# An attention and experts block on one core: another layout for a weighted sum, and another order in its drain

## The reference

```
y    = clip(modulated_linear(x), -256, 256)              # weights scaled by the batch's condition
x1   = x + (y + attention(y))                            # 16 heads of 64, 4 groups of keys and values
kx   = modulated_linear(x1)                              # reshaped to 16 heads of 8 features
A    = softmax(kx kx^T / sqrt(8))                        # within one token: 16 x 16 over the heads
tok  = modulated_linear(A kx)
out  = x1 + sum over the top 2 of 8 experts of gate_e * (relu(tok W1_e + b1_e) W2_e + b2_e)
```

## Time and profile before

| | |
|---|---|
| median of 3 runs | 598.16 us (595.11 to 598.86) |
| the profiled execution | 596.94 us, span 595.1 us |
| busy in the span | PE 575.1, PEld 492.3, DVE 483.7, ACT 372.0, POOL 288.1 us |
| one steady slot | 14.17 us (pair begins at 298.63 and at 312.80) |
| slots 33 and 34, routing, first expert | from about 480 to 514.80 us |
| experts | 514.80 us to the end |

### The profile page before, as it was taken

How to read it: one execution, slowest core, us unless ns; L and a number is a source line. 1 busy time by engine, 2 the same in 40 slices (tenths; PEclk the granted TensorE clock), 3 DMA queues, 4 the chain that set the end, 5 groups by cost and what they waited for, 6 DMA issues and landing times. The chain is left out here.

```text
span 595.1 us, 15251 instructions
## 1 busy us (share of the span) xinstructions
PE 575.1 (97%) x4516; PEld 492.3 (83%) x4516; DVE 483.7 (81%) x1026; ACT 372.0 (63%) x855; POOL 288.1 (48%) x248
## 2 busy tenths in 40 slices
PE   8999999999999999999999999999998997799998
PEld 8888888888888888888888888888887896466775
DVE  4235888898989898988889898989898788777776
ACT  1767767777777677777777767777775321534443
POOL 1011666666666666666666666666666563000000
PEclk9999999999999999999999999999999977999999
DMA  7300000000000000000000000000000000000004
GB/s 240 86 2 2 1 3 2 0 0 0 0 0 0 0 0 0 0 0 0 0 0 0 0 0 0 0 0 0 0 0 2 1 1 0 1 1 0 0 0 141
DMA packets 9364, 7.18 MB, mean 12 GB/s; under 512 B 1089, under 2 KB 8833, under 8 KB 9217
## 3 DMA queue, kind: packets, MB, share of 16 engines
q1 hardware_dynamic: 9344, 6.94, 3.9%
HBM read 4.84 MB, written 2.10 MB: 12 GB/s over the span
## 5 line engine op out<-in xcount | busy, mean ns | idle before, releaser
L1068 POOL TENSOR_TENSOR pair<-kx 128x1152 f32<-128x1152 f32 x32 | 82.2, 2568 | 167.4 <-DVE shifted L388 158.4
L580 PE MATMUL bank_a<-v,prob 128*128 128x65 f32 x1024 | 128.5, 274 | 1.5 <-ACT prob L814 0.8
L580 PEld LDWEIGHTS bank_a<-v,prob 128*128 128x128 f32 x1024 | 121.8, 192 | 6.3 <-ACT prob L814 3.2
L1063 POOL TENSOR_TENSOR mix_hi<-mix_hi 128x512 f32<-128x512 f32 (+2 forms) x96 | 116.8, 1217 | 7.5
L271 DVE TENSOR_REDUCE row_max<-bank_s 128x4 bf16<-128x512 f32 x128 | 88.9, 694 | 26.2 <-PE bank_s L555 25.3
L814 ACT ACTIVATE prob<-bank_t 128x512 f32<-128x512 f32 x128 | 68.9, 589 | 6.9 <-PE bank_t L570 4.7
L587 PE MATMUL misc<-yT,wq_sb 128*128 128x128 f32 x512 | 69.6, 279 | 0.5 <-DVE yT L419 0.5
L570 PE MATMUL bank_t<-qT,kT 64*128 64x256 f32 x512 | 65.7, 376 | 0.0
L1056 POOL TENSOR_TENSOR mix_hi<-weight,kx 128x1024 f32<-128x1024 f32 x32 | 64.1, 2002 | 3.1 <-ACT weight L814 3.1
L282 DVE TENSOR_TENSOR att<-bank_a,recip_den 128x256 f32<-128x256 f32 x128 | 54.4, 425 | 13.0
L587 PEld LDWEIGHTS misc<-yT,wq_sb 128*128 128x128 f32 x512 | 62.0, 191 | 3.6 <-DVE yT L419 0.7
(11 more groups left out here) (149 smaller groups left out, 998.9 us busy)
## 6 DMA issues: line engine op xcount, KB each, us to landing
out<-acc_all SPq DMA_DIRECT2D x8, 256.0 KB, 2.3
x_all<-in_xT SPq DMA_DIRECT2D x1, 1024.0 KB, 9.7
w_sb<-in_w SPq DMA_DIRECT2D x2, 512.0 KB
x_all<-in_xT SPq DMA_DIRECT2D x1, 768.0 KB, 7.5
wq_sb<-in_wq SPq DMA_DIRECT2D x1, 512.0 KB, 6.1
wpost_sb<-in_wpost SPq DMA_DIRECT2D x1, 512.0 KB, 9.6
x_all<-in_xT SPq DMA_DIRECT2D x1, 256.0 KB, 3.3
b_rows<-in_b SPq DMA_DIRECT2D x16, 4.0 KB
```

The lines of the kernel that those rows point to most:

```text
L580: last = mm(att_bank(g)[:, w, :], prob[:, g % 2, w, :], v1[:, j, g, :], start=(w == 0), stop=True, skip_group_check=True)
L1063: G.tensor_tensor(mix_hi[:, 0:r, :], mix_hi[:, 0:r, :], mix_hi[:, r:2 * r, :], ALU.add).then_inc(s_hi, 1)
L1068: G.tensor_tensor(pair[:, :, :], bass.AP(kx2, jc * 2 * P, [[4 * P, P], [0, SHIFTS], [1, P]]), bass.AP(kx2, jc * 2 * P, [[4 * P, P], [MD, S ...
```

## The change

On VectorE the product of the mixing is written transposed: `mix_lo` is now laid out as (feature, shift), so that the 8 terms of one sum lie next to each other and each write is 8 floats behind the last. One reduction over them (`mix_part`) takes the place of the three additions. GpSimd's `mix_hi` gets two buffers, and its product waits for the mix_sum of two batches before instead of one.

In the late slots VectorE does the scores of h first, and copies them itself with two reductions of length 1 (`own_copies`) where ScalarE had two copies. The first choice of the early tiles moves from slot 33 to slot 34, behind the last mixing, and ScalarE's route_exp with it; the second choice of the early tiles is no longer made apart, but with the recent ones over all 32. Of TensorE's fillers, keep_going(12) in slot 34 becomes keep_going(4), and three keep_going(3), in slots 33 and 34, go away; keep_going(40) in slot 33 stays.

```diff
-        mix_lo = sb("mix_lo", [P, MH // 2, P])
-        mix_hi = sb("mix_hi", [P, MH // 2, P])
+        mix_lo = sb("mix_lo", [P, P, MH // 2])
+        mix_part = sb("mix_part", [P, P])
+        mix_hi = sb("mix_hi", [P, 2, MH // 2, P])
...
-                    V.tensor_tensor(mix_lo[:, :, :].rearrange("p r (h e) -> p r h e", e=MD),
+                    V.tensor_tensor(mix_lo[:, :, :].rearrange("p (h e) r -> p r h e", e=MD),
                                     weight[:, jd, 0:MH // 2, :].unsqueeze(3).to_broadcast([P, MH // 2, MH, MD]),
                                     bass.AP(kx2, jd * 2 * P, [[4 * P, P], [MD, MH // 2], [MD, MH], [1, MD]]),
                                     ALU.mult).then_inc(s_lo, 1)
                 if D:
-                    dve.wait_ge(s_lo, 4 * d + 1)
-                    V.tensor_tensor(mix_lo[:, 0:4, :], mix_lo[:, 0:4, :], mix_lo[:, 4:8, :], ALU.add).then_inc(s_lo, 1)
+                    dve.wait_ge(s_lo, 2 * d + 1)
+                    V.tensor_reduce(mix_part[:, :], mix_lo[:, :, :], AX.X, ALU.add).then_inc(s_lo, 1)
...
-                    V.tensor_tensor(mix_lo[:, 0:2, :], mix_lo[:, 0:2, :], mix_lo[:, 2:4, :], ALU.add).then_inc(s_lo, 1)
-                    V.tensor_tensor(mix_lo[:, 0, :], mix_lo[:, 0, :], mix_lo[:, 1, :], ALU.add).then_inc(s_lo, 1)
...
+                def own_copies():
+                    if H:
+                        dve.wait_ge(s_score, n(h))
+                        V.tensor_reduce(score[:, 1:MH // 2, MH:2 * MH], score[:, 1:MH // 2, 0:MH].unsqueeze(3), AX.X,
+                                        ALU.max).then_inc(s_twice, 1)
+                        dve.wait_ge(s_twice, n(h))
+                        top = MH // 2 - 1
+                        V.tensor_reduce(score[:, SHIFTS:MH, 0:MH],
+                                        bass.AP(score, top * (2 * MH - 1) + MH,
+                                                [[2 * MH * MH, P], [-(2 * MH - 1), top], [1, MH], [1, 1]]),
+                                        AX.X, ALU.max).then_inc(s_mirror, 1)
+
                 if late(s):
                     head_scores()
+                    own_copies()
                     head_shift()
-                    mixed()
-                    if s == BATCH + 2:
-                        second_choice(EARLY, 1)
...
-                if s_is(s, BATCH + 1):
+                if s_is(s, BATCH + 2):
                     dve.wait_ge(s_log, 1)
                     dve.wait_ge(s_const, 3)
                     first_choice(EARLY)
...
-            second_choice(RECENT, 2)
+            second_choice(range(BATCH), 2)
...
                     if s_is(s, BATCH + 2):
-                        keep_going(12)
+                        keep_going(4)
...
-                if late(s):
-                    keep_going(3)
...
                 if s_is(s, BATCH + 2):
-                    keep_going(3)
                     gate_logits(RECENT[-1:])
...
                 if late(s):
-                    head_copies()
                     head_weights()
-                if s_is(s, BATCH + 1):
-                    route_exp(EARLY)
...
                     f(mixT[:, :], misc[2][:, 0, :], scale=style[:, 2, bass.ds(d, 1)]).then_inc(s_mixT, 1)
+                if s_is(s, BATCH + 2):
+                    route_exp(EARLY)
...
-                    need(pool, s_msum, n(d - 1))
+                    need(pool, s_msum, n(d - 2))
```

## The result

The changed kernel takes 606.89 us (median of 4 runs, 606.2 to 609.13), the one before 598.09 us. The ratio is 1.0164, with a 95% interval of 1.0139 to 1.019: slower by 1.6%, and outside the predicted range. The profiled execution took 606.25 us, with a span of 604.4 against 595.1.

A forecast was written before the change was run, and what follows sets the result against it. TensorE was taken to bound the loop, and a chain over VectorE the drain. Loop 0, drain -3.8 and clock +1.6 gave -2.2 us, so 596.0 us from a median of 598.16; range 592.3 to 603 for 8 in 10 runs.

The forecast's parts named there:

- part 1: VectorE's mixing: rows written next to each other, one 1.21 us reduction for additions of 2.67 us, gaining VectorE 1.46 us a slot.
- p = 0: VectorE's product: p is the extra time for writing with a step of 8 floats, taken as 0, range 0 to 0.76 us.
- The first rival: VectorE's product in every slot: strided writes are slow, TensorE waits from p = 0.55 us; 603.8 us at 0.76, chance 0.25.
- slack of 0.15 us: Steady slot: prob's first half ends at 307.9, TensorE needs it at 308.20, leaving about 0.15 us after the hand-over.
- The loop's gain: Steady slots: VectorE's saving hardly shows because GpSimd's half becomes late; put at 0, from nothing to 0.05 us a slot.
- The drain: Late slots: new order and shorter sum end mix(31) at 496.9 instead of 501.37, a gain of 4.5 us.
- From mix(31) to count: Transposition, logits and routing after the last mixing: 6.9 to 7.5 us instead of 6.70, so 0.2 to 0.8 lost.
- the net up to count: Drain up to the routing's count: the earlier mix(31) less the longer routing, a net gain of 3.8 us.
- The clock: Experts: with fewer fillers TensorE may start at half clock for 0 to 6.8 us, costing 0 to 3.2, taken as 1.6.
- the loop as a gain: Loop: rival that TensorE did wait for VectorE, 0.2 us a slot, total 590.4 us; chance 0.08.
- a drain without effect: Drain: rival that mix(31) is no earlier and a cold start eats the rest, 598 to 600 us; chance 0.08.
- the forecast's own case: Whole kernel with p = 0: the product's write costs nothing extra, time 596.0 us; chance 0.42 for 594.3 to 598.

The follow-up runs named there:

- the experiment with x_all first: Changed kernel with the new x_all placed between VectorE's product and its reduction, against the kernel before: 598.05 us, ratio 1.0008.
- pairs: Changed kernel with two shifts next to each other, product written with a step of 2 floats, against the kernel before: 596.7 us, ratio 0.9983.
- the drain alone: Changed kernel with the product and three additions of before turned back, against the kernel before: 597.09 us, ratio 0.9988.
- the old order with the reduction: Kernels with the drain order of before and the one reduction; the one with only the new layout and reduction took 605.5 us, ratio 1.0139.
- old order with x_all first: Kernel before with the transposed product, the one reduction and x_all between them, nothing of the new drain order: 596.27 us, ratio 0.9979.
- both kernels with idle fillers and x_all first: Eleven fillers where TensorE waits, added to the x_all-first kernels, against the kernel before: new drain order 596.75 us, old order 595.72 us.

## Why the prediction was wrong

**The step that failed** is in part 1: "I take p = 0 and keep 0.76 for the range." The trace had one pair of rows on accesses of this step, the reductions of the earlier trace rows, and they gave 0.76 us. I set them aside because they are reads, and had no row that says that writes are different. They are not: 2.00 against 1.23 us alone, so p = 0.77, and 0.81 in the loop (2.32 against 1.51), at and above the top of my 0 to 0.76. The rule that I cited spoke on the same side. The nearest row should have been the value, and "it is a write" the reason for the other end.

**The first rival was right in its place and too small in its price.** It named the chain x_all, x1s, prob, and the experiment with x_all first shows that this is the way. It had TensorE waiting from p = 0.55 on, 0.22 us a slot at 0.76, 6.3 us in all. The slot grew by 0.35 and the 30 slots by 9.3. The place was the only one, but the slack of 0.15 us in front of it was mis-read: by the weight load it was 0.03, as worked out above, and that tenth in 29 slots is about the 3 us by which its total of 603.8 was short. Its sign, x1s that delays prob, is what the trace has; TensorE's busy share, 99.38 for 99.58, hardly showed it.

**The loop's gain** of 0 to 0.05 us a slot for the 1.46 us that VectorE would save with a fast product is right: 14.08 before, 14.09 with the sum at full speed. mix_sum waits for GpSimd instead, as said.

**The drain.** Forecast 4.5 us for mix(31) with p = 0. Measured from the last pair product it is 3.34 in the changed kernel, where two slow products cost 1.6, and 4.8 with pairs. With the slot ahead of it (12.44 us before, 11.98 with pairs) it is 5.3: near, and on the safe side. The blocks by GpSimd fell where I had laid them. From mix(31) to count, forecast 0.2 to 0.8 us longer, measured 1.31. The transposition starts 0.53 us after mix(31), as forecast, and from the logits to count it is 4.42 us, as forecast (1.16 + 3.2). From the transposition to the logits it is 3.05 us at half clock, where I had the 2.39 of before; I had put the price of the clock on the experts alone. With pairs the net up to count is 26.8 - 23.4 = 3.4 us, and 3.9 with the slot ahead, where I had 3.8.

**The clock.** Forecast 1.6 us at the experts for a cold stretch of 0 to 6.8; the stretch came, 3.4 us long, and cost 1.4: the first expert matmul to the first addition of its result is 7.85 us against 6.45. The other 1.0 of the 2.39 isn't the clock (last section). Why the experts begin at half clock here is open: in the kernel with x_all first, where TensorE has the same instructions, they begin at full clock (6.44 us).

**The rivals that fell**: the loop as a gain, and a drain without effect.

**Luck in the forecast's own case.** 596.7 us with pairs lies near 596.0, but the terms don't all agree. The 1.6 us for the clock at the experts did not come there (6.45 us to the first addition), and 1.0 us that nobody had forecast, at full clock, stood in its place. By the stages of the trace the kernel with pairs gains 2.5 us behind the first pair product; the medians give 0.9.

## What to carry to other kernels

Before a transposed write is put on a path that counts, work out how many elements share 16 bytes: two float32 in a line are free, one alone in its line costs 0.62 to 0.75 ns more on VectorE here, reading or writing, and a layout in pairs keeps both sides at full speed. When an engine of 99% busy is the bound, look at the count of its instructions in a stretch and not at its busy time, and at everything that stands behind the edited instructions on their own engine: the loss came through an addition of 0.28 us that the change didn't touch. When you read a slack in front of a matmul, read it to the load of its weights. A row that gives a price for the nearest thing is the value to take; only another row is a reason to take zero.

## What the runs showed that I had not expected

The experts' stage has the same instructions in all kernels, and still takes 80.3 us before and in the drain alone, 80.9 in the old order with the reduction, and 81.3 in the new order with it. In the kernel with pairs the clock is full over it:

```profile
521.00:560.00 39.00, 38.40 (x211) 26.73 (x212) 27.64 (x86) 16.97 (x33) 0.00 (x0) 1.00 0.00 0
```

The chain that ended last goes over TensorE there before (bank_t 6% of the span, VectorE's acc_all 0%). After, most of it does too, but VectorE's additions and its sequencer (DVEq) have 1% each:

```profile
PE bank_t L783 5%; PE misc L791 3%; PE bank_s L791 2%; DVE acc_all L489 1%; DVEq L489 1%; DVE acc_all L477 0%; PE misc L617 0%; PE bank_a L533 0%; PE misc L725 0%; DVE mix L342 0%; PE bank_a L775 0%; ACT tok_all L818 0%; ACT mixT L818 0%; ACTq L998 0%; ACT hT L818 0%
```

The times of the single additions are the same, 351 ns. In the trace VectorE's first instruction behind the loop's branch comes 0.23 us after the branch instead of 0.14. Only the code ahead of the loop differs, so its place in memory is one guess; no run tested it, and the cause stays open.

And the start of the kernel scatters, though the code is the same up to there except for the mixing: the first pair product begins between 41.4 and 41.7 us in four traces (old order with x_all first, both kernels with idle fillers and x_all first, pairs), and between 43.2 and 44.5 in the others. Those four profiled executions lie 1.3 to 4.3 us below the median of their kernel, the others from 1.4 below to 2.1 above. So a difference of two profiled spans, or of two medians by a microsecond or two, says less than the stages do.
